# Masking the diagonal score tiles in place in PSUM: one maximum from PSUM, then ScalarE's copy

## The reference

```
xn = layernorm(x)
q, k, v = split(xn @ W_qkv)
scores = where(key later than query, -inf, q @ k.T / 16)
attn = softmax(scores) @ v
x + attn + shared_swiglu(xn) + routed_swiglu(xn)[top-1 expert of 32]
```

## Time and profile before

| | |
|---|---|
| median of 3 runs | 2272.65 us |
| the profiled execution, own time | 2279.66 us |
| its span | 2277.7 us |
| TensorE busy | 2235.3 us (98%) |
| VectorE busy | 1642.8 us (72%) |
| ScalarE busy | 1160.2 us (51%) |
| GpSimd busy | 1071.2 us (47%) |
| mean granted TensorE clock | 0.995 |

### The profile page before, as it was taken

The page is one execution under the profiler, slowest core; times in us unless marked ns, Lnnn a source line. Parts: engine busy times, 40 slices in busy tenths (PEclk is TensorE's granted clock), DMA queues, the critical chain, the costliest instruction groups (busy, mean ns, idle before and its releaser), DMA issues.

```text
span 2277.7 us, 46624 instructions
## 1 busy us (share of the span) xinstructions
PE 2235.3 (98%) x15254; PEld 2060.5 (90%) x15254; DVE 1642.8 (72%) x3543; ACT 1160.2 (51%) x2190; POOL 1071.2 (47%) x1016
## 2 busy tenths in 40 slices
PE   8999999999998999999999999999999999999997
PEld 7888888888888999999999997999998989898987
DVE  7777777777778977878788865766676766666665
ACT  4334344434435656666556554555555555555544
POOL 2323323333333434444344434666666666666665
PEclk9999999999999999999999999999999999999999
DMA  7665665566547877787777775243434343434330
GB/s 252 212 211 197 204 221 198 193 229 208 167 145 244 268 251 251 250 261 259 251 251 254 254 223 161 94 147 123 140 128 135 125 137 126 137 123 137 131 107 29
DMA packets 299531, 423.16 MB, mean 186 GB/s; under 512 B 35777, under 2 KB 216002, under 8 KB 299330
## 3 DMA queue, kind: packets, MB, share of 16 engines
q1 hardware_dynamic: 281986, 384.48, 50.2%
q0 software_dynamic: 17344, 36.27, 5.9%
HBM read 281.92 MB, written 138.74 MB: 185 GB/s over the span
## 4 chain that ended last, share of the span: by engine, by line
PE 94%; DVE 3%; issue 1%; ACT 1%; DMA 1%; SPq 0%; POOL 0%; ACTq 0%; DVEq 0%
PE ahead_psS L87 11%; PE ahead_psS L88 10%; PE ahead_psS L89 10%; PE ahead_psX L87 7%; PE ahead_psX L89 7%; PE ahead_psX L88 7%; PE t_psO L1748 6%; PE t_psO L1750 6%; PE t_psO L1752 6%; PE e_psG L87 3%; PE e_psG L88 3%; PE e_psG L89 3%; PE a_psD L89 3%; PE a_psD L87 3%; PE a_psD L88 3%; PE a_psT L87 1%
## 5 line engine op out<-in xcount | busy, mean ns | idle before, releaser
L1550 POOL TENSOR_TENSOR t_p_lo<-t_score,t_p_hi 128x512 fp32r<-128x512 f32 (+1 forms) x320 | 359.6, 1129 | 215.2 <-ACT t_score L1679 114.9
L1671 ACT COPY t_score<-ahead_psS 128x512 f32<-128x512 f32 (+3 forms) x288 | 148.4, 516 | 334.9 <-PE ahead_psS L89 317.0
L1748 PE MATMUL t_psO<-t_v_hi,t_p_hi 128*128 128x258 f32 x1088 | 315.0, 290 | 3.5 <-DVE ahead_dout L1636 3.5
L1750 PE MATMUL t_psO<-t_v_hi,t_p_lo 128*128 128x258 f32 x1088 | 308.8, 284 | 0.0
L1752 PE MATMUL t_psO<-t_v_lo,t_p_hi 128*128 128x256 f32 x1088 | 307.6, 283 | 0.0
L1067 POOL DMA_INDIRECT ahead_rows<-xs_rows,ahead_slot x144 | 177.2, 1230 | 211.4 <-PE e_psT L1247 166.4
L354 POOL DMA_INDIRECT token_of<-a_token_i,a_slot_i x128 | 140.6, 1099 | 244.8 <-DVE a_slot_i L465 206.9
L87 PE MATMUL ahead_psS<-ahead_q_hi,ahead_x_hi 128*128 128x512 f32 (+3 forms) x640 | 235.1, 367 | 6.8 <-DVE ahead_q_lo L1577 3.5
L88 PE MATMUL ahead_psS<-ahead_q_hi,ahead_x_lo 128*128 128x512 f32 (+3 forms) x640 | 234.2, 366 | 0.0
L89 PE MATMUL ahead_psS<-ahead_q_lo,ahead_x_hi 128*128 128x512 f32 (+3 forms) x640 | 233.6, 365 | 0.0
L1748 PEld LDWEIGHTS t_psO<-t_v_hi,t_p_hi 128*128 128x128 f32 x1088 | 207.3, 191 | 11.6 <-DVE ahead_dout L1636 4.1
(11 more groups left out here) (266 smaller groups left out, 7183.2 us busy)
## 6 DMA issues: line engine op xcount, KB each, us to landing
ahead_raw<-in_L_ffn_routed_gate_w SPq DMA_DIRECT2D x42, 512.0 KB
ahead_raw<-in_L_ffn_routed_up_w SPq DMA_DIRECT2D x42, 512.0 KB
ahead_raw<-in_L_ffn_routed_down_w SPq DMA_DIRECT2D x41, 512.0 KB
e_raw<-in_L_ffn_routed_gate_w SPq DMA_DIRECT2D x41, 512.0 KB
e_raw<-in_L_ffn_routed_up_w SPq DMA_DIRECT2D x41, 512.0 KB
e_raw<-in_L_ffn_routed_down_w SPq DMA_DIRECT2D x41, 512.0 KB
a_xt<-in_L_attn_x SPq DMA_DIRECT2D x32, 512.0 KB, 5.9
v_high<-a_v_hi SPq DMA_DIRECT2D x32, 512.0 KB, 3.8
```

What stands on the lines that cost most here:

```text
L1550: g_.tensor_tensor(p_lo[:, t % LR, c0:], score[:, t % SR, c0:], p_hi[:, t % HR, c0:].bitcast(F32), ALU.subtract).then_inc(lo_ok, 1)
L1671: s.copy(score[:, t % SR, c0:], psS[:, n % BANKS, c0:]).then_inc(u_act, 1)
L1748: nc.tensor.matmul(psO[:, a, 0:W], p_hi[:, kp, cols], v_hi[:, kv, j % J], start=j == 0, stop=False, skip_group_check=True)
L1750: nc.tensor.matmul(psO[:, a, 0:W], p_lo[:, t % LR, cols], v_hi[:, kv, j % J], start=False, stop=False, skip_group_check=True)
```

## The change

On a diagonal tile VectorE waits for the matmuls alone, adds the mask to `own` in place in PSUM, waits for that write, and takes one maximum over the tile's whole width from PSUM (for j = 0 one copy). ScalarE's copy to `score` now covers the tile's whole width and waits for that maximum. The counts of `Plan` follow: one read and one write of `top`, and one copy, for each diagonal tile.

```diff
@@ -1379,12 +1379,11 @@
                 n += 1
             self.s_unit.append(n)
             _, G, j = self.tiles[t]
-            diagonal, rest = self.diagonal(t), self.cut(t) < J - 1
-            tops = self.tops[-1] if t else 0
-            self.reads.append(tops + (rest if diagonal else j > 0))
-            self.tops.append(self.reads[t] + diagonal)
+            diagonal = self.diagonal(t)
+            self.reads.append((self.tops[-1] if t else 0) + (diagonal or j > 0))
+            self.tops.append(self.reads[t])
             self.diags.append((self.diags[-1] if t else 0) + diagonal)
-            self.acts.append((self.acts[-1] if n else 0) + (rest or not diagonal))
+            self.acts.append((self.acts[-1] if n else 0) + 1)
             n += 1
         self.splits = {n: k + 1 for k, n in enumerate(self.split)}
 
@@ -1584,23 +1583,16 @@
                 if j == 0 and G > 0:
                     return
                 if plan.diagonal(t):
-                    own, c1 = slice(c0, c0 + P), c0 + P
+                    own = slice(c0, c0 + P)
                     wait(dve, u_mm, n + 1)
-                    wait(dve, u_act, plan.acts[n])
-                    wait(dve, lo_ok, t - SR + 1)
-                    v.tensor_tensor(score[:, t % SR, own], s[:, own], keep.mask[:], ALU.add).then_inc(diag_ok, 1)
+                    v.tensor_tensor(s[:, own], s[:, own], keep.mask[:], ALU.add).then_inc(diag_ok, 1)
+                    wait(dve, diag_ok, plan.diags[t])
                     if j == 0:
                         wait(dve, top_mm, g - TR + 1)
-                        v.tensor_copy(m[:, c1:], s[:, c1:]).then_inc(top_ok, 1)
+                        v.tensor_copy(m[:], s).then_inc(top_ok, 1)
                     else:
                         wait(dve, top_ok, plan.tops[t - 1])
-                        if c1 < GT:
-                            v.tensor_tensor(m[:, c1:], m[:, c1:], s[:, c1:], ALU.max).then_inc(top_ok, 1)
-                    wait(dve, diag_ok, plan.diags[t])
-                    if j == 0:
-                        v.tensor_copy(m[:, own], score[:, t % SR, own]).then_inc(top_ok, 1)
-                    else:
-                        v.tensor_tensor(m[:, own], m[:, own], score[:, t % SR, own], ALU.max).then_inc(top_ok, 1)
+                        v.tensor_tensor(m[:, c0:], m[:, c0:], s[:, c0:], ALU.max).then_inc(top_ok, 1)
                     return
                 wait(dve, u_act, plan.acts[n])
                 if j < 2:
@@ -1663,11 +1655,12 @@
 
             def keep_score(t):
                 n = plan.s_unit[t]
-                c0 = (plan.cut(t) + plan.diagonal(t)) * P
-                if c0 == GT:
-                    return
+                c0 = plan.cut(t) * P
                 wait(act, lo_ok, t - SR + 1)
-                wait(act, u_mm, n + 1)
+                if plan.diagonal(t):
+                    wait(act, top_ok, plan.tops[t])
+                else:
+                    wait(act, u_mm, n + 1)
                 s.copy(score[:, t % SR, c0:], psS[:, n % BANKS, c0:]).then_inc(u_act, 1)
 
             def exps(t):
```

## The result

| | before | after |
|---|---|---|
| median | 2272.0 us (2271.22 to 2278.24, 4 runs) | 2296.49 us (2295.99 to 2302.5, 4 runs) |
| profiled execution | 2279.66 us | 2302.5 us |
| its span | 2277.7 us | 2300.6 us |
| VectorE busy | 1642.8 us (72%) | 1591.7 us (69%) |

The account below looks back on a forecast made before the run. TensorE, busy 98% of the span, was taken to bound the kernel. Terms 8.4 + 6.3 + 4.2 + 1.9 - 2.0 - 3.5 = +15.3 us on 2272.65 gave 2288.0 us; range 2276 to 2300, some 8 in 10.

Parts of the forecast that it names:

- (d): ScalarE's queue behind the waiting copy, then VectorE's next mask and maximum: later units miss their bank, 14 x 0.3 = 4.2 us.
- (a): TensorE's three waits of 0.66 us each for `top`, behind the SBUF maximum L1603, go: -2.0 us.
- (b): Kernel's end: the 0.79 us output-line wait and part of the 4.6 us wait behind L1603 go, -3.5 us.
- L1603 is long because of GpSimd: VectorE's maximum of two SBUF buffers waits for a port while GpSimd reads SBUF; the worst one runs 6.06 us.
- within 10 ns: Sign to look for: the new diagonal maxima, at every width, take within 10 ns of L1612 and L1598.
- Mask to maximum 0.38 start to start: On VectorE at diagonal tiles, the maximum that waits for the mask starts 0.38 us after the mask starts.
- Bank late, 14 x 0.60 = 8.4: First diagonal tile of 16-tile and 8-tile groups: score bank released 0.60 us later in 14 places, 8.4 us.
- Turn places, 14 x 0.45 = 6.3: First tile of 4-tile groups and first diagonal tile of 12-tile groups, 7 each: 0.45 us later, 6.3 us.
- (c): Kernel's start: TensorE's 1.89 us wait for bank 0 shrinks, -0.8 us, and perhaps a 1.2 GHz stretch goes, 1.6 more.
- (e): First 25 steps, without weighing as cover: +2.1 us in group 1, +0.6 in group 2, +1.6 for a 1.2 GHz stretch.
- Rival 3: ScalarE's queue becomes the bound, exponentials waiting behind each diagonal copy: +26.8 us, 2299 us; chance 0.17.
- Rival 1: Removed waits win: VectorE comes earlier to each diagonal mask and the chain mask-maximum-copy fits, -11.4 us, 2261 us; chance 0.06.

Follow-up runs that it names:

- run 7: The kernel before, with GpSimd's subtraction for the low part of p replaced by a memset to zero: 2261.05 us, ratio 0.9945.
- run 12: The kernel before, with the change only on second to fourth diagonal tiles from the second sequence on, and the negated row maximum written to PSUM: 2261.08 us.
- run 1: The kernel after, with ScalarE's two exponentials ahead of its copy in the step of a diagonal tile: 2282.78 us, ratio 1.0043.
- Runs 2 and 3: The kernel before, with the change only on each group's first diagonal tile (2302.66 us), or only on the other three (2271.22 us).
- run 4: The kernel before, mask still to SBUF, but ScalarE's copy behind VectorE's maximum of the rest from the fifth tile on: 2293.53 us, ratio 1.0094.
- run 3: The kernel before, with the change only on the second to fourth diagonal tile of each group: 2271.22 us, ratio 0.9992.

## Why the prediction was right, and where not

Sign and mechanism held; the loss was 9 us larger than the likeliest value. That it was no more is in part luck: in the profiled executions the places of the bank, the turns, (d) and the start came out 13.3 us above their terms, and (a) and (b) 5.4 us below, most of that from what varies at the end. By its terms:

- **L1603 is long because of GpSimd**: shown by run 7, and for the spread tile by run 12. The mask in PSUM at 284 ns: 291. The maxima lie 2 to 12 ns above those of L1612 and L1598, so the sign "within 10 ns" was just missed for 128 and 256 columns (288 and 422 ns). Mask to maximum 0.38 start to start: 0.32 (1435.57 to 1435.89), against 0.20 for the old pair without the wait. What the Trainium skill says ("VectorE: DVE Perf Modes", section "The DRAIN you can't avoid"), that the semaphore costs nothing extra, it measured on a chain of eight copies. It is not borne out for this pair, and would have taken the forecast further from the time measured.
- **Bank late, 14 x 0.60 = 8.4**: 14 x 0.62 = 8.7. Right.
- **Turn places, 14 x 0.45 = 6.3**: 7 x 0.57 and 7 x 1.04 = 11.3. The failed half is that of the 4-tile groups. There the spread tile ahead of the mask takes 1.17 us, because GpSimd, fed by the later exponentials, now reads just then:

```profile
1448.32 1.30 POOL L1549 TENSOR_TENSOR t_p_lo<-t_score,t_p_hi 128x512 fp32r<-128x512 f32 x1
...
1449.01 1.17 DVE L1612 TENSOR_TENSOR t_spread<-keep_ident,t_negmax 128x512 fp32r<-128x512 f32 x1
```

  With the exponentials first (run 1) the spread tile takes 0.69 and the same place costs 0.57. Runs 2 and 3 tell that it is the waiting copies of the second to fourth diagonal tile that shift GpSimd. I had moved VectorE and ScalarE in time, but left GpSimd where it was.
- **(d), 14 x 0.3 = 4.2**: 14 x 0.60 = 8.4, and another 1.4 in small ones. This step failed in size and in place. I followed the banks through the four tiles ("0 us", then misses of 0.1 and 0.2) and not the output line, which stands behind L1577 on VectorE's queue although it has nothing to do with it. Run 1 removes these 14 and keeps the 14 of the bank; run 4 has them in full with the bank only 0.26 late.
- **(a), -2.0**: -2.4. Right.
- **(b), the end, -3.5**: everything from 2160 on gives -8.5 against the first profiled execution and -3.3 against the second. Of this 1.8 us are another place, in both: at 2162 the spread tile took 3.55 us before and takes 0.69 after. The place that (b) means, output line and stall together, gives -1.8 and -1.4 us, half of its term and near its end of -1. For the stall moves to the spread tile, as (b) feared: in the kernel after

```profile
2257.12 2.50 POOL L1549 TENSOR_TENSOR t_p_lo<-t_score,t_p_hi 128x512 fp32r<-128x512 f32 x2
...
2257.30 4.77 DVE L1612 TENSOR_TENSOR t_spread<-keep_ident,t_negmax 128x512 fp32r<-128x512 f32 x1
...
2262.12 0.80 PE L1727 MATMUL ahead_psX<-t_spread,t_ones 128*128 128x512 f32 x1 [4.15 <-DVE t_spread L1612]
```

  it makes TensorE wait 4.15 us where L1603 made it wait 4.6.
- **(c) and (e), the start, +1.9**: +4.3, inside the ends of -1 and +5. TensorE's wait for bank 0 fell from 1.89 to 1.04 us, as worked out. The stretch at 1.2 GHz from 1359 did not go, and a new one came from 1376: windows of the kernel after,

```profile
1359.00:1362.00 3.00, 3.00 (x9) 2.34 (x8) 0.00 (x0) 0.60 (x2) 0.00 (x0) 0.51 0.01 3
...
1376.00:1380.00 4.00, 3.78 (x12) 3.08 (x12) 0.68 (x3) 2.47 (x7) 1.70 (x2) 0.57 1.09 348
```

  so the 1.6 us that I had saved in (c) was not there. The rest of the difference is the late ScalarE queue of group 1; with the exponentials first the start is 5.6 us better.

Rival 3, ScalarE's queue as the bound (2299), had the better number, 2.5 us off against 8.5 for the forecast, and part of its mechanism; but it let that queue work through exponentials that GpSimd and the weighing want. They ran far enough ahead; the part of the queue that counted was L1662 (L1654 after). Its number is luck in part too: its (d), 12.6 us against 9.8, covers for the turn places, which it had 5.0 too low. Rival 1 was told apart by run 3: the gains it names exist (turns, end) and come without the cost where the first diagonal tile stays as it was.

Not settled: why the clock falls behind the same 1.9 us of idle time in one execution and not in the other. Not tried: a third buffer for the output rows in the kernel of run 12, which by its profile still loses about 3 us to a landing and the slow stretch behind it.

## What to carry to other kernels

An instruction that is made to wait for another engine delays all that stands behind it in its queue, and the next engine's queue after that; follow each of these to the first thing TensorE needs, however unrelated, and move the engines that are fed by it in time as well. A second wait need not shrink with the first: here it was 0.60 us behind a first one of 0.62 and behind one of 0.26. An instruction that is long because another engine reads SBUF is worth curing where it makes the bound engine wait: 2 kinds of places here gave 12 us, while the change took 51 us from VectorE's busy time and the kernel still got longer.

## What the runs showed of the hardware that I had not expected

- In these runs a VectorE instruction all of whose tensors are in SBUF was held up while GpSimd read SBUF, be it a maximum of two tiles (749 ns in the mean against 286), a copy of one (839 against 218) or a tensor-scalar of one (up to 3.3 us against 0.28). Beside a GpSimd memset it was not (run 7, 26 of 26), nor with one input in PSUM (run 12, 32 of 32 at 686 to 690 ns). It can be held through several GpSimd instructions in a row, for 6.06 and 4.77 us, where single ones take 0.7 to 1.3.
- The same kernel met an output row that landed 1.9 us late, and a stretch at 1.2 GHz behind an idle time of 1.9 us, in one execution and not in the other; the spans are 6.1 us apart. A single profile's end is thus no measure of a term of a few us.
